# VectorE's flag and base loads moved behind the one-hots, and one branch and one tick for a pair of groups, in a two-layer graph network

## The reference

```python
h = jnp.maximum(_layernorm(x, axis=-1), 0.0)
x = x + _L0_gnn_ref(h, src, dst, edge_weight, L0_gnn_W, L0_gnn_b)
h = jnp.maximum(_layernorm(x, axis=-1), 0.0)
x = x + _L1_gnn_ref(h, edge_attr_64, W_msg, b_msg, W_upd, b_upd, eps, src, dst)
# L0: segment_sum(w * (h @ W + b)[src], dst) / (segment_sum(w, dst) + 1e-6), then relu
# L1: gelu(((1 + eps) * h + segment_sum(gelu([h[src], e] @ W_msg + b_msg), dst)) @ W_upd + b_upd)
```

## Time and profile before

| What | Value |
|---|---|
| runs | 2679.41, 2669.0, 2678.9 us; median 2678.9 us |
| span of the profiled execution, first to last instruction | 4082.0 us |
| its own time | no other than its span is known |
| instructions in it | 72599 |
| busy in it: PE, PEld, DVE, ACT, POOL | 2950.6, 2600.4, 2089.7, 1607.4, 1835.1 us |
| mean granted TensorE clock in it | 0.844 |
| layer 0 in it | about 105 to 1824 us |
| layer 1 in it | about 1878 to 4057 us |

### The profile page before, as it was taken

How to read it: one execution, slowest core, us unless ns; L and a number is a source line. 1 busy time by engine, 2 the same in 40 slices (tenths; PEclk the granted TensorE clock), 3 DMA queues, 4 the chain that set the end, 5 groups by cost and what they waited for, 6 DMA issues and landing times.

```text
span 4082.0 us, 72599 instructions
## 1 busy us (share of the span) xinstructions
PE 2950.6 (72%) x22325; PEld 2600.4 (64%) x22326; DVE 2089.7 (51%) x4376; ACT 1607.4 (39%) x5144; POOL 1835.1 (45%) x1911
## 2 busy tenths in 40 slices
PE   2776766665665666576788788778878878878887
PEld 2666665554554555565677677677767767767777
DVE  8444445544544554544455455555545545555554
ACT  2343333433433443334344444444434444444443
POOL 2333344334434434424455545545545554554552
PEclk9888787877777777787888888888888888888888
DMA  4000000000000000002333333333333333333332
GB/s 92 14 12 14 13 16 16 13 13 15 14 12 15 15 13 14 15 14 66 75 84 85 81 81 84 87 79 83 88 76 86 83 81 81 84 87 78 85 88 52
DMA packets 473123, 214.39 MB, mean 53 GB/s; under 512 B 264996, under 2 KB 442024, under 8 KB 473076
## 3 DMA queue, kind: packets, MB, share of 16 engines
q1 hardware_dynamic: 412404, 151.55, 14.2%
q0 software_dynamic: 60672, 62.25, 9.2%
HBM read 208.14 MB, written 5.51 MB: 52 GB/s over the span
## 4 chain that ended last, share of the span: by engine, by line
PE 41%; issue 11%; another core or an unknown queue 1%; DVE 1%; DVEq 0%; ACT 0%; ACTq 0%
PE ps L918 28%; PE ps L1123 6%; PE ps L988 5%; PE ps L1112 2%; DVE sel L1451 0%; PE ps L1070 0%; DVE rows L1455 0%; DVEq L1464 0%; PE ps L1017 0%; ACT eT L844 0%; DVE sums_sb L1472 0%; DVE parts L1219 0%; DVE room L1654 0%; ACT dw L652 0%
## 5 line engine op out<-in xcount | busy, mean ns | idle before, releaser
L629 POOL DMA_INDIRECT rows<-p_table,idx x1176 | 1109.4, 943 | 1065.6 <-ACT idx L660 736.0
L918 PE MATMUL ps<-parts,pick_all 128*128 128x448 f32 x5488 | 1241.0, 379 | 63.5 <-issue 59.9
L629 POOL DMA_INDIRECT rows<-h_table,idx x720 | 709.5, 985 | 1062.1 <-ACT room L760 857.7
L918 PEld LDWEIGHTS ps<-parts,pick_all 128*128 128x128 f32 x5488 | 1046.3, 195 | 193.6 <-issue 109.4
L947 PE MATMUL ps<-adj,h_sb 128*64 128x160 f32 (+1 forms) x4802 | 503.4, 342 | 516.4 <-issue 469.9
L947 PEld LDWEIGHTS ps<-adj,h_sb 128*64 128x64 f32 x4802 | 404.4, 170 | 608.8 <-issue 551.9
L1451 DVE TENSOR_TENSOR sel<-ps,mask 128x896 f32<-128x896 f32 x196 | 213.5, 1089 | 761.4 <-remote 541.9
L1388 DVE TENSOR_SCALAR hot_p<-iota_p,scal 128x256 fp32r<-128x256 f32 (+1 forms) x848 | 309.4, 365 | 410.9 <-PE ps L928 321.6
L928 PE MATMUL ps<-hot_c,hot_p 128*128 128x125 f32 (+1 forms) x2336 | 456.3, 302 | 87.6 <-issue 72.4
L721 ACT COPY adj<-ps 128x500 f32<-128x500 f32 (+1 forms) x848 | 389.8, 524 | 203.0 <-PE ps L928 126.5
L928 PEld LDWEIGHTS ps<-hot_c,hot_p 128*128 128x128 f32 x2336 | 377.4, 207 | 110.5 <-issue 86.5
(11 more groups left out here) (181 smaller groups left out, 2975.9 us busy)
## 6 DMA issues: line engine op xcount, KB each, us to landing
src_all<-keys SPq DMA_DIRECT2D x196, 448.0 KB
ea<-in_edge_attr_dram SPq DMA_DIRECT2D x196, 256.0 KB
rows<-p_table,idx POOLq DMA_INDIRECT x1176
rows<-h_table,idx POOLq DMA_INDIRECT x720
x_sb<-in_x_dram SPq DMA_DIRECT2D x6, 224.0 KB, 3.5
h_table<-h_sb SPq DMA_DIRECT2D x6, 224.0 KB
p_table<-h_sb SPq DMA_DIRECT2D x6, 224.0 KB
out_dram<-h_sb SPq DMA_DIRECT2D x6, 224.0 KB
```

The costliest lines, as they stand in the source:

```text
L629: nc.gpsimd.indirect_dma_start(out=rows[:, s, j, 0:D], out_offset=None, in_=table[:, :], in_offset=bass.IndirectOffsetOnAxis(ap=idx[:, s, ...
L918: last = nc.tensor.matmul(to, hot[:, k, t * P:(t + 1) * P], parts[:, part, k, :, :].rearrange("p a d -> p (a d)"), start=(k == 0 and part ...
```

## The change

On VectorE, `sums` of one group becomes `pair_sums` of two: both adds come first, then one branch on the two flags together, in which the further windows of either group stand behind a branch of their own (`more_sums`, whose body is as before, with the wait on `s_acc` set to the pair's last add), then one tick of two elements that adds 2 to `s_done`. On TensorE the further windows of a pair stand behind one outer branch in both layers. In layer 0 VectorE no longer loads the flags at the start of a body and the bases one by one ahead of the sums: right behind the two one-hots of a pair it loads, for slots 0 and 1, the flags and both bases, and for slots 2 and 3 both bases. In layer 1 the loads stay where they are.

```diff
 # TensorE, first (layer 0); second (layer 1) likewise
-                    for r in (s - 1, s):
-                        more_windows(0, b, r, lambda j, r=r: wrows[r][:, j, :], DA, 1, more, here)
+                    with pe.If((more & (3 << (s - 1))) > 0):
+                        for r in (s - 1, s):
+                            more_windows(0, b, r, lambda j, r=r: wrows[r][:, j, :], DA, 1, more, here)
 # VectorE
-            def sums(layer, b, s, width, base, more, z=None):
...
+            def pair_sums(layer, b, s, width, bases, more, z=None):
+
+                par = (s - 1) % 2
+                for i, r in enumerate((s - 1, s)):
+                    dve.wait_ge(s_win[layer], b * SLOTS + (r + 1))
+                    dve.wait_ge(s_acc[layer], b * SLOTS + (r + 2))
+                    to = sums_sb[0:width, bass.ds(bases[i], WIN)]
+                    nc.vector.tensor_tensor(to, to, psW[(par + i) % 2][0:width, :], ALU.add).then_inc(s_acc[layer], 1)
+                with dve.If((more & (3 << (s - 1))) > 0):
+                    for i, r in enumerate((s - 1, s)):
+                        with dve.If((more & (1 << r)) > 0):
+                            more_sums(layer, b, r, width, bases[i], psW[(par + i) % 2], s, z)
+                nc.vector.memset(tick[:, s - 1:s + 1], 0.0).then_inc(s_done, 2)
...
             def first(b, here, ahead, further):
-                more = more_flags(b)
...
                             onehots(0, r, s_oh[0], here)
+                        if s == 0:
+                            more = more_flags(b)
+                        bases = base_of(b, s), base_of(b, s + 1)
                     if s < 2 and ahead:
                         build(ahead, b + 1, s + 2)
...
-                    if s % 2 == 0:
-                        base0 = base_of(b, s)
-                    else:
-                        base1 = base_of(b, s)
-                        sums(0, b, s - 1, DA, base0, more, here)
-                        sums(0, b, s, DA, base1, more, here)
+                    if s % 2:
+                        pair_sums(0, b, s, DA, bases, more, here)
...
 # VectorE, second (layer 1)
-                        sums(1, b, s - 1, P, even, more)
-                        sums(1, b, s, P, odd, more)
+                        pair_sums(1, b, s, P, (even, odd), more)
```

More of the change, by code:

```diff
@@ L1150, in second @@
                     if s % 2:
-                        for r in (s - 1, s):
-                            more_windows(1, b, r, lambda j, r=r: msgs[r][:, j * D:(j + 1) * D], D, 2, more)
+                        with pe.If((more & (3 << (s - 1))) > 0):
+                            for r in (s - 1, s):
+                                more_windows(1, b, r, lambda j, r=r: msgs[r][:, j * D:(j + 1) * D], D, 2, more)
             with pe.Fori(0, BODIES - 1) as b:
@@ new lines, in more_sums @@
+            def more_sums(layer, b, r, width, base, summed, last, z):
+                g = b * SLOTS + r
+                count = dve.value_load(row_i[0:1, bass.ds(g, 1), 1], min_val=1, max_val=MAXW)
+                before = dve.value_load(row_i[0:1, bass.ds(g, 1), 2], min_val=0, max_val=MAXW * NG)
+                dve.wait_ge(s_acc[layer], b * SLOTS + (last + 3))
+                dve.sem_inc(s_passed, 1)
+                with dve.Fori(0, count - 1) as i:
+                    k = before + i + 1
+                    n = J if layer else z.JH + 1
+                    nc.vector.tensor_scalar_add(dw[:, r, 0, 0:n], dw[:, r, 0, 0:n],
+                                                -float(WIN)).then_inc(s_more_dw[layer], 1)
+                    dve.wait_ge(s_more_dw[layer], k)
+                    onehots(layer, r, s_more_oh[layer], z)
+                    dve.wait_ge(s_more_win[layer], k)
+                    at_node = nc.s_assert_within(base + i * WIN + WIN, 0, N - 1, skip_runtime_bounds_check_because=(
+                        "a group has just enough windows to reach its greatest target, which is below N"))
+                    to = sums_sb[0:width, bass.ds(at_node, WIN)]
+                    nc.vector.tensor_tensor(to, to, summed[0:width, :], ALU.add).then_inc(s_more_acc[layer], 1)
+                    dve.wait_ge(s_more_acc[layer], k)
```

## The result

The changed kernel takes **2706.05 us** (median of 4 runs, 2703.75 to 2712.98), the kernel before on the same chip 2674.8 (4 runs, 2669.0 to 2679.41): ratio 1.0135, 95% interval 1.0112 to 1.0159, so slower by 31 us (1.2%) in the medians and by 1.4% in the ratio. The forecast was 2722, slower. The times of most versions here, the kernel before among them, lie in two groups some 12 us apart, so versions within 10 us of each other are compared by their lower groups too (what was seen of the upper one is told last).

What follows compares the result with a forecast made beforehand. VectorE's sequence was taken to bound layer 0 and TensorE layer 1. Moved loads add 26.0 us in zone 1 and 17.3 in zone 0, branch and tick 0: 2678.9 + 43 = 2722 us, own range 2700 to 2745.

Steps and rivals of the forecast that it cites:

- The stalls are the recording's: Long TensorE and VectorE waits in the 4082.0 us profiled execution come from recording; unrecorded runs have next to none.
- The price of a load, 0.65: VectorE's sequencer, layer 0: an uncovered register load with its register steps costs 0.65 us.
- Dear loads: Rival on VectorE's loads in layer 0: each costs 0.89 us, giving 2756 us; chance 3%.
- Builds pass the loads: Rival on VectorE in layer 0: queued builds run past the loads, -62 us, giving 2617; chance 3%.
- Short loads: Rival on VectorE in layer 0: unrecorded loads cost less and are covered, giving 2671 to 2659 us; chance 14%.
- Zone 1, +0.84 a body: Layer 0's later bodies, 31 counted: VectorE gains 2.13 us idle behind one-hots and loses 0.65 and 0.64, net +0.84.
- Zone 0, +1.08 a body: Layer 0's 16 bodies of zone 0: moved loads on VectorE cost 1.54 + 0.89 - 0.65 - 0.70, net +1.08 us.
- the sum of 2648: Whole kernel before, rebuilt without stalls from preparation, both layers and the end: 2648 us, 1.2% under the median.
- The sum: Layer 0's total cost of the moved loads: 26.0 us in zone 1 plus 17.3 in zone 0, +43 us.
- TensorE's chain is the longer one: Rival, layer 0, build release through windows and adjacency sums to next release: exceeds 21.2 us, giving 2648; chance 12%.
- Gathers bind: Rival on GpSimd in layer 0: a gather takes over 1.33 us and sets the pace, giving 2679 us; chance 13%.
- Branch and tick, 0: VectorE's shared branch and tick and TensorE's outer branches, both layers: taken to change the time by 0.

Runs made afterwards that it cites:

- e0: The kernel before, unchanged, profiled again: 2670.78 us, profile span 2669.0 us, without the long stalls.
- e4: The changed kernel with one more base load, its value unused, behind each pair's loads (two a body): 2772.76 us, ratio 1.0368.
- e7: The kernel before with flags and slot 0's base loaded behind the body's first build, plus two unused base loads there: 2635.26 us, ratio 0.9855.
- e2: The kernel before with only its layer 0 loads moved behind the one-hots, branches and ticks unshared: 2715.87 us, ratio 1.0196.
- e3: The kernel before with its flags and slot 0's base loaded behind the body's first build: 2627.7 us, ratio 0.9866.
- e1: The changed kernel with the loads back in their old places, branch and tick still shared: 2681.11 us (12 runs), ratio 1.0034.
- e8: The changed kernel with the loads back in their old places, run a second time: 2674.26 us (12 runs), ratio 1.0014.
- e6: The kernel before with only TensorE's outer branches added, in both layers: 2670.3 us (12 runs), ratio 0.9997.

## Why the prediction was right, and where it was off

- **The stalls are the recording's:** right (e0). But the forecast that the profile of the changed kernel would span 4082 us within 1% failed, 2703.4: I took the recording to stall again because it had stalled once. That the one recording showed VectorE's idle times at their true price all the same (1.17 and 0.56 in it, 1.18 and 0.56 in e0) was not known beforehand.
- **The price of a load, 0.65:** right. e4 gives 0.63 of idle time without any model, and 0.73 by the body. Dear loads are out, and the price holds in unrecorded runs as well: by e4's median the two loads cost 67 us, 31 x 1.46 = 45 of them by zone 1's body, the rest in zone 0.
- **Builds pass the loads:** out. The Trainium skill, "Advanced Engine Details and Errata", section Sequencer Loop, lets other instructions be read and queued meanwhile. This case's traces don't agree for VectorE's loads: in e4 no arithmetic came past, at 0.63 a load, and in e7 only what was queued *before* the loads ran on over them.
- **Short loads:** out. The Trainium skill, "Runtime: NRT & Kernel Launch", section Instruction fetch mechanics, gives about 200 ns a register for TENSOR_LOAD, there in the runtime's own sequences. The instruction takes 0.29 here, and with its register steps VectorE's path pays 0.63.
- **Zone 1, +0.84 a body:** right, +0.79 measured. The idle times came where they were put: 1.17 to 0.44 (forecast 0.53), 0.56 to none, 0.77 (0.74) and 1.46 (1.39). Round 21.2, measured 21.38. That VectorE sets this pace is shown both ways: idle time added lengthens the body (e2, e4), taken out shortens it (e3) until the gathers bind.
- **Zone 0, +1.08 a body, the step that was off.** The sentence "16 x 16.3" took VectorE's round and the gathers as the only candidates, and never added up TensorE's work there: 17.16 us, more than 16.3 (16 x 0.8 = 13 of the 21 us by which the sum of 2648 falls short of the span of 2669). The same omission is in "in layer 0 TensorE has slack", which set its branches at 0. In zone 0 TensorE had none: the loads made it wait for its windows, and behind that wait two branches cost 0.2 more than one (e2). So the loads alone cost 1.06 a body (18.19 against 17.13), and the sharing, set at 0, gave 0.28 back: +0.78. That 1.06 is so near to the forecast 1.08 is luck, since it came about on TensorE's path. VectorE's tiles show the bound too, if more than two of them are read: before, `hot_p` has a mean of 393 ns in this stretch, because some last 0.49 to 0.56 us where the others last 0.34; I read that as waiting for TensorE within the instruction. It is 403 in e3, where VectorE has time to spare, and 369 after the change. The rows in 154 to 360 us, before and after:

```profile
L1388 DVE TENSOR_SCALAR hot_p<-iota_p,scal 128x256 f32<-128x256 f32 (+1 forms) x236 | 92.8, 393 | 9.2 <-PE ps L928 9.2
```
```profile
L1390 DVE TENSOR_SCALAR hot_p<-iota_p,scal 128x256 f32<-128x256 f32 x230 | 84.8, 369 | 29.8 <-PE ps L928 26.4 <-ACT scal L656 3.3
```

- **The sum:** 37 instead of 43 by the bodies, 31 by the medians. Zone 0 accounts for 5 of the 12 us missing, by what the sharing gave back there, and zone 1 for 1.5. The rest, some 6, is not located: the spans differ by 34.4, the medians of four runs by 31. For the loads alone the sum was nearer: 41 by the bodies and 47 by the medians of e2.
- **TensorE's chain is the longer one** (12%): out for zone 1, since the body grew by 0.79 where this rival took 0.64 off, and e3 shortens it by 1.5. In zone 0 TensorE did set the pace, and there I had not reckoned it.
- **Gathers bind** (13%): not in the kernel before, but they are only some 1.2 us below VectorE's round (20.2 against 21.38), and e3 reaches them in zone 1's last bodies.
- **Branch and tick, 0:** right with the loads in their old places (e1, e8, e6), not beside the moved loads, where the sharing gave some 10 us back (e2 against the changed kernel). Part of it is TensorE's branch in zone 0; what VectorE's branch and tick gave was not separated.

## What to carry to other kernels

A register load on VectorE's sequencer cost nothing here while arithmetic queued before it was still running, and its whole price, 0.63 us, where it stood between a short operation and the next work: place it behind the longest run of queued operations, not behind the instruction that is nearest in the source. Branches behaved alike on TensorE: the second of two was free where products were queued ahead of it, and cost 0.2 us behind a wait. Sum every engine's own work in every stage before calling one of them the bound, and take more than one period of the trace for it. Where a gap's releaser changes from body to body, suspect the sequencer, and count its steps by adding one.

## What the hardware showed that was not expected

**TensorE's clock fell where VectorE's gaps made it wait.** In 450 to 900 us, zone 1, the granted clock was 1.00 before and 0.96 after (the windows above), 0.95 in e2, 0.93 in e4 and 1.00 in e3. Stretches of the changed kernel ahead of one fall and in it, columns as above:

```profile
706.00:711.00 5.00, 2.34 (x23) 2.13 (x20) 4.09 (x13) 4.07 (x13) 3.78 (x5) 1.00 0.13 26
...
712.00:713.00 1.00, 1.00 (x11) 1.00 (x10) 1.00 (x5) 0.00 (x0) 0.91 (x1) 0.50 0.17 33
```

TensorE had stood 3.04 us ahead of its windows; then they ran at 0.50, the 1.2 GHz level, and took 2.63 us instead of 1.41 in a pair without such a wait:

```profile
711.38 2.63 PE L988 MATMUL ps<-onehot,room 128*65 128x72 f32 x20 [3.04 <-DVE room L1431]
718.03 1.41 PE L988 MATMUL ps<-onehot,room 128*65 128x72 f32 x20
```

Before, the same wait was 1.8 us at the longest and the clock stayed at 1.00. The length of the wait alone doesn't decide it: in e1, with 0.98 in this stretch, windows behind a wait of 1.86 took 2.41 us, and in e6 the longest wait was 1.9 and the clock stayed at 1.00. What this adds to a body was not separated from the loads.

**The two groups of times.** In one profiled execution of an upper group (e7: 2644.93 us, its other runs 2634.65 to 2635.3) TensorE worked at half the granted clock from 2612 us to its end at about 2639; the kernel before (second profile, lower group) had 1.00 at that place. The two, e7 first:

```profile
2606.00:2612.00 6.00, 4.21 (x67) 3.82 (x65) 3.65 (x6) 0.63 (x1) 0.00 (x0) 1.00 0.00 0
2612.00:2618.00 6.00, 5.62 (x28) 5.58 (x29) 0.86 (x3) 0.58 (x1) 0.00 (x0) 0.52 0.02 4
```
```profile
2650.00:2656.00 6.00, 5.58 (x53) 5.58 (x54) 2.05 (x5) 1.15 (x2) 0.00 (x0) 1.00 0.02 4
```

Busy as long, TensorE does 28 products there instead of 53. Just before it had stood idle for 6.00 - 4.21 = 1.8 us of six; the kernel before had stood idle for 1.4 of six (4.56 busy in 2644 to 2650 us) and kept its clock. From the last L1451 to VectorE's last operation e7 takes 33 us (2605.82 to 2638.61) and the kernel before 20 (2644.18 to 2664.47): that is the distance of the two groups. Why the clock falls in one execution and not in another stays open, and no other run of an upper group was profiled.
